# Semaphore waits between the indirect transfers of a mixture-of-experts layer on one core: the scatter waits at every second transfer, the closing gather at every tile

## The chip, the cores and the metric

The kernel runs on one core of one Trainium2 chip. The metric is the device time of one execution in microseconds (us). The engines are TensorE (PE, with its weight loads shown apart as PEld), VectorE (DVE), ScalarE (ACT), GpSimd (POOL) and SyncE (SP), which here only starts transfers.

## What is computed

One transformer layer over 2048 tokens of width 512: sparse and windowed attention, a layer norm, then a mixture of experts with a shared part, and a second layer norm. The change lies in the mixture of experts. Its reference, cut to what matters:

```python
scores = sigmoid(xf @ gate_w.T) + expert_bias          # 16 experts, 4 groups, best 2 groups kept
_, idx = top_k(masked, 4)                               # four experts per token
w = take_along_axis(original_scores, idx); w = w / sum(w)
h = silu(einsum('td,edh->teh', xf, w1)) * einsum('td,edh->teh', xf, w3)
y = einsum('teh,ehd,te->td', h, w2, cw)                 # routed experts
z = silu(xf @ sw1) * (xf @ sw3) @ sw2                   # shared experts
x = layernorm(x + y + z)
```

The kernel doesn't compute every expert for every token: it sorts the tokens by expert, computes only the picked ones and gathers the results back.

## The kernel before

The activations stand in SBUF as `acc`, 16 token tiles (NT) of 128 tokens by 512 numbers. The feed-forward part has three blocks, with a barrier of all engines after each.

**The shared experts and the routing (block that ends at line 1029).** Two shared experts of three row blocks each make six steps q per chunk c of 512 tokens (four tiles); chunks 0 to 2 are done here, numbered m = 6c + q. For each step TensorE computes two products of 12 matmuls (`up`), ScalarE a silu (line 1183), VectorE (for chunk 0 GpSimd) the product of both (`hidden`, line 1020), ScalarE and VectorE its split into a high and a low part (lines 1196 and 1026), and TensorE the third product of 12 matmuls (`down`) one step later. TensorE may not start the second half of `up` of step m before `hidden` of step m - 1 is done. Meanwhile VectorE works out the routing, and ends with `slots` (line 1352): for each token the four rows of a DRAM buffer `xs` to which it goes. Then GpSimd scatters: for each tile n and pick k, one indirect transfer (line 1229) writes the 128 rows of `acc[:, n, :]` to `xs`, 64 transfers of 256 KB. They count on one semaphore per chunk, `s_scat[0]` to `s_scat[3]`, 16 each. These wait for it:

- VectorE, before it may change `acc` of a chunk that is being sent: for chunk 0 in steps q = 2 to 5 of chunk 1 (line 1370), behind `hidden` of that step and ahead of the next one, and for chunks 1 and 2 at the end of the chunk (line 1375);
- SP, for all four, before it loads the first sorted tile (line 1049);
- GpSimd itself, for all four, before the barrier.

**The routed experts (block that ends at line 1447).** Loops over tiles of sorted tokens, expert by expert; results go to the DRAM buffer `ys`.

**The close (`combine`, block that ends at line 1651).** GpSimd gathers the four result rows of each token, four indirect transfers of 256 KB per tile (line 1716), into one of NG = 6 buffers `got`; they count on the buffer's semaphore `s_got`. VectorE adds them to `acc`, weighted (line 1762), and takes mean and variance (lines 1767 to 1771). GpSimd then raises the variance to the power -1/2 (`power`, line 1722), VectorE makes the bias of the norm from it (`less_mean`, line 1736), ScalarE applies both (line 1696) and SP stores the tile. In the same block TensorE, ScalarE and VectorE compute the shared experts of the last chunk, six steps (`late_block`) beside tiles 1 to 6, whose results VectorE adds at tiles 12 to 15 (line 1756). GpSimd's order sets the pace, since `power` stands behind gathers that run six tiles ahead, and VectorE takes tile n + 2 only after `power(n)`:

```python
for n in range(NT):
    gather(n)
    if n >= NG:
        power(n - NG)
for n in range(NT - NG, NT):
    power(n)
```

Of the kernel before, what the change touches and what calls it, by code (L numbers as in the profile page):

```python
# [31 lines left out]
TPC = CH // P  # L32
# [11 lines left out]
PICK = 4  # L44
# [892 lines left out]
def front(nc, t, bank, acc, ident, xs, zeroed, slots, pick_w, tile_expert, first_tile, neghalf, x, x_in,  # L937
# [7 lines left out]
    with st:  # L945
# [33 lines left out]
        s_scat = [sem(f"scatter_done{c}", st) for c in range(NCH)]  # L979
# [12 lines left out]
        def piece(i):  # L992

            return (i // QUARTERS + 1) % RING, quarter(i % QUARTERS)
# [16 lines left out]
        def hidden(eng, m):  # L1011
            rows = rows_of(m)
            eng.wait_ge(s_silu, m + 1)
            wait_hlo(eng, m - 1)
            if m < POOL_BLOCKS:
                eng.wait_ge(s_u3c, m + 1)
                eng.tensor_tensor(hid[0:rows, :], gate[0:rows, :], up3[0:rows, :], ALU.mult).then_inc(s_hid_pool, 1)
            else:
                eng.wait_ge(s_u3, m + 1)
                eng.tensor_tensor(hid[0:rows, :], gate[0:rows, :], b_u3[0:rows, :], ALU.mult).then_inc(s_hid_dve, 1)  # L1020

        def hidden_low(eng, m):
            rows = rows_of(m)
            wait_hid(eng, m)
            eng.wait_ge(s_hhi, m + 1)
            eng.tensor_tensor(hlo[0:rows, m % 2, :], hid[0:rows, :], hhi[0:rows, m % 2, :].bitcast(F32),
                              ALU.subtract).then_inc(s_hlo_pool if m < POOL_BLOCKS else s_hlo_dve, 1)

        with nc.Block() as block:
            @block.sync  # L1030
            def _(sp):
                def load_piece(i):
                    if i >= QUARTERS:
                        sp.wait_ge(s_wlo, i - QUARTERS + 1)
                    e = (E, E + 1, 0, 1)[i // QUARTERS]
                    q = i % QUARTERS
                    sp.dma_start(staged[:, quarter(q)], t["wexp"][e, :, quarter(q)]).then_inc(s_piece[q], 16)

                sp.dma_start(gateT[:, :, :], t["gateT"].rearrange("(k p) e -> p k e", p=P)).then_inc(g_in, 16)
                for i in range(QUARTERS):  # L1040
                    load_piece(i)
                sp.dma_start(ebias[:, :], t["ebias"].broadcast_to([P, E])).then_inc(g_in, 16)
                sp.dma_start(tri, t["tri"]).then_inc(g_in, 16)
                sp.dma_start(ramp[:, :], t["ramp"].broadcast_to([P, MAXT])).then_inc(g_in, 16)
                for i in range(QUARTERS, PIECES + QUARTERS):
                    load_piece(i)
                for c in range(NCH):
                    sp.wait_ge(s_scat[c], 16 * TPC * PICK)
                sp.dma_start(x[:, :], xs[P:2 * P, :]).then_inc(x_in, 16)
# [158 lines left out]
            @block.gpsimd  # L1208
            def _(pool):
                def piece_low(i):  # L1210
                    s, cols = piece(i)
                    pool.wait_ge(s_whi, i + 1)
                    pool.tensor_tensor(wlo[:, s, cols], staged[:, cols], whi[:, s, cols].bitcast(F32),
                                       ALU.subtract).then_inc(s_wlo, 1)

                pool.memset(neghalf[:, :], -0.5)
                for i in range(2 * QUARTERS):
                    piece_low(i)
                for m in range(POOL_BLOCKS):
                    hidden(pool, m)  # L1220
                    hidden_low(pool, m)
                    if m < QUARTERS:
                        piece_low(2 * QUARTERS + m)
                pool.wait_ge(s_slots, 1)
                for z in zeroed:
                    pool.wait_ge(*z)
                for n in range(NT):
                    for k in range(PICK):
                        pool.indirect_dma_start(xs[:, :], bass.IndirectOffsetOnAxis(ap=slots[:, n, k:k + 1], axis=0),
                                                acc[:, n, :], None, bounds_check=MAXT * P - 1,  # L1230
                                                oob_is_err=False).then_inc(s_scat[n // TPC], 16)
                for c in range(NCH):
                    pool.wait_ge(s_scat[c], 16 * TPC * PICK)

# [387 lines left out]
def combine(nc, t, bank, acc, ident, ys, slots, pick_w, mv, rstd, neghalf, stats, whi, wlo, staged, sb, sem):  # L1622
# [3 lines left out]
    with st:  # L1626
        NG = 6
# [11 lines left out]
        s_got = [sem(f"got{i}", st) for i in range(NG)]  # L1639
# [11 lines left out]
        with nc.Block() as block:  # L1651
            @block.tensor
            def _(pe):
                for k in range(KC):
                    wait_for(pe, s_xlo, k - 1)
                    for i in range(TPC):
                        mm = pe.transpose(bank[k % 2][:, i * P:(i + 1) * P], acc[:, LATE + i, k * P:(k + 1) * P],
                                          ident[:, :])
                    mm.then_inc(s_xt, 1)
                pe.wait_ge(s_xlo, KC)  # L1660
                for q in range(NB):
                    s, b = divmod(q, HB)
                    rows = hb_rows(b)
                    wait_for(pe, s_hid, q - 1)
                    for w in range(2):
                        for k in range(KC):
                            at = w13_cols(w, k)[0] + b * P
                            mm = three_products(pe, bank[2 + 2 * w + q % 2][0:rows, :],
                                                (whi[:, slot(s), at:at + rows], wlo[:, slot(s), at:at + rows]),
                                                (xhi[:, k, :], xlo[:, k, :]), k == 0, k == KC - 1)  # L1670
                    mm.then_inc(s_up, 1)
                pe.wait_ge(s_hlo, NB)
                for i in range(TPC):
                    cols = slice(i * P, (i + 1) * P)
                    for q in range(NB):
                        s, b = divmod(q, HB)
                        rows = hb_rows(b)
                        lo_, hi_ = w2_cols(b)
                        mm = three_products(pe, b_y[i][:, :], (hhi[0:rows, q, cols], hlo[0:rows, q, cols]),
                                            (whi[0:rows, slot(s), lo_:hi_], wlo[0:rows, slot(s), lo_:hi_]),  # L1680
                                            q == 0, q == NB - 1)
                    mm.then_inc(s_y, 1)
# [27 lines left out]
            @block.gpsimd  # L1710
            def _(pool):
                def gather(n):
                    if n >= NG:
                        pool.wait_ge(s_sum, PICK * (n - NG + 1))
                    for k in range(PICK):
                        pool.indirect_dma_start(got[n % NG][:, k, :], None, ys[:, :],  # L1716
                                                bass.IndirectOffsetOnAxis(ap=slots[:, n, k:k + 1], axis=0),
                                                bounds_check=MAXT * P - 1, oob_is_err=False).then_inc(s_got[n % NG], 16)

                def power(n):  # L1720
                    pool.wait_ge(s_eps, n + 1)
                    pool.tensor_tensor(rstd[:, n:n + 1], rstd[:, n:n + 1], neghalf[:, :], ALU.pow).then_inc(s_pow, 1)  # L1722
# [7 lines that stand above are left out]
# [105 lines left out]
```

## Time and profile before

| | us |
|---|---|
| median of 2 runs | 2546.36 (2545.96 to 2546.77) |
| profiled execution | 2546.89 |
| its span, first to last instruction | 2545.1 |
| scatter: first issue to end of the last | 1678.2 to 1759.9 |
| start of the routed experts | 1839.1 |
| close: first gather to end of the last | 2422.0 to 2514.2 |

The profiled execution took 0.5 us more than the median, and 1.8 us of it lie outside the span. Times in the trace count from the span's start. Busy time of an engine leaves out semaphore waits, branches and the time that a transfer takes after its issue. TensorE's matmuls are pipelined, and their ends are modelled. A bracket at the end of a row of the timeline gives the idle time of the engine before the row and what released it; "issue" and "remote" there mean that the profile shows no releaser.

### The profile page before, as it was taken

How to read it: one execution, taken by the hardware profiler on the slowest of the kernel's cores; microseconds unless marked ns; L12 is line 12 of the kernel's file. 1: busy time of each engine (PE TensorE's matmuls, PEld its weight loads, DVE VectorE, ACT ScalarE, POOL GpSimd, SP SyncE). 2: the span in 40 equal slices, each digit the busy share in tenths (PEclk: the TensorE clock that was granted, in tenths of full speed). 3: DMA queues.
4: the chain of work that ended last, by engine and by line, in shares of the span. 5: the costliest groups of instructions: out<-in, count | busy, mean ns of one | idle time of the engine just before them, and what ended most of it. 6: DMA issues, size and time to landing. Idle time of an engine off the chain costs nothing. (4 is left out here: it accounts for less than half of the span.)

```text
span 2545.1 us, 45306 instructions
## 1 busy us (share of the span) xinstructions
PE 2249.2 (88%) x13489; PEld 2022.1 (79%) x13490; DVE 1372.0 (54%) x4446; ACT 1172.1 (46%) x3726; POOL 1345.5 (53%) x1942
## 2 busy tenths in 40 slices
PE   5399999999999999999999997773999999878763
PEld 3299999899899898998999986652789998767642
DVE  4266666667666666766666682830323323343247
ACT  2166666566566665665666664310123333333211
POOL 2576666666666666666666663455011103463374
PEclk9699999999999999999999996785999999989876
DMA  3230250000000000000000002233033324554264
GB/s 117 78 150 4 79 209 18 5 20 18 5 20 20 19 4 21 18 6 19 20 18 3 1 2 74 71 124 145 30 119 109 114 78 141 173 190 139 93 180 150
DMA packets 68916, 178.29 MB, mean 70 GB/s; under 512 B 11648, under 2 KB 15296, under 8 KB 68672
## 3 DMA queue, kind: packets, MB, share of 16 engines
q1 hardware_dynamic: 36864, 85.58, 10.1%
q0 software_dynamic: 19568, 69.10, 8.3%
q10 hardware_dynamic: 12240, 20.73, 2.2%
q8 instruction: 106, 1.74, 0.3%
q14 instruction: 138, 1.13, 0.2%
HBM read 108.26 MB, written 67.13 MB: 69 GB/s over the span
## 5 line engine op out<-in xcount | busy, mean ns | idle before, releaser
L773 POOL TENSOR_TENSOR cross<-nat,rope_tables 128x128 f32<-128x128 f32 x256 | 147.9, 578 | 447.1 <-DVE nat L635 447.1
L921 PE MATMUL bank<-whi,xT_lo 128*128 128x384 f32 x1024 | 369.6, 361 | 2.5 <-ACT v L727 1.7
L922 PE MATMUL bank<-wlo,xT_hi 128*128 128x384 f32 x1024 | 347.8, 340 | 0.0
L923 PE MATMUL bank<-whi,xT_hi 128*128 128x384 f32 x1024 | 346.8, 339 | 0.0
L1473 POOL TENSOR_TENSOR ring_lo<-staged,ring_hi 128x1088 fp32r<-128x1088 f32 x48 | 121.2, 2538 | 404.9 <-ACT ring_hi L1435 401.2
L597 DVE TENSOR_TENSOR acc<-acc,bank 128x512 f32<-128x512 f32 x256 | 175.8, 687 | 227.5 <-PE bank L923 210.3
L707 ACT COPY probT<-bank 128x128 f32<-128x128 f32 (+3 forms) x256 | 109.1, 426 | 380.8 <-PE bank L549 380.8
L921 PE MATMUL bank<-ring_hi,xslo 128*128 128x352 f32 x600 | 204.1, 340 | 29.3 <-issue 27.9
L635 DVE TENSOR_TENSOR nat<-bank,bqk 128x256 f32<-128x256 f32 x256 | 108.8, 425 | 166.3 <-PE bank L923 165.1
L921 PEld LDWEIGHTS bank<-whi,xT_lo 128*128 128x128 f32 x1024 | 193.7, 189 | 3.1 <-DVE nat L635 1.9
L923 PE MATMUL bank<-ring_hi,xshi 128*128 128x352 f32 x600 | 195.7, 326 | 0.0
L922 PE MATMUL bank<-ring_lo,xshi 128*128 128x352 f32 x600 | 195.2, 325 | 0.0
L922 PEld LDWEIGHTS bank<-wlo,xT_hi 128*128 128x128 f32 x1024 | 194.2, 190 | 0.0
L923 PEld LDWEIGHTS bank<-whi,xT_hi 128*128 128x128 f32 x1024 | 193.2, 189 | 0.0
L578 PE MATMUL bank<-probT,cv 128*128 128x128 f32 x1280 | 185.0, 275 | 3.1 <-ACT probT L709 3.1
L774 POOL TENSOR_TENSOR roped<-nat,rope_tables 128x256 f32<-128x256 f32 x256 | 181.7, 710 | 0.0
L1601 DVE TENSOR_TENSOR shlo<-bank,shhi 128x256 fp32r<-128x256 f32 x76 | 32.2, 424 | 275.7 <-ACT shhi L1567 275.7
L782 POOL TENSOR_TENSOR rstd<-ssq,half 128x2 f32<-128x2 f32 x256 | 180.5, 705 | 0.0
L716 ACT ACTIVATE prob<-prob,nbias,rstd 128x256 f32<-128x256 f32 (+1 forms) x256 | 152.7, 597 | 59.3 <-DVE nbias L622 48.4
L578 PEld LDWEIGHTS bank<-probT,cv 128*128 128x128 f32 x1280 | 163.0, 192 | 3.8 <-ACT probT L709 3.8
L539 PE MATMUL bank<-ckT,qkT 128*128 128x160 f32 (+15 forms) x512 | 161.9, 398 | 0.0
L763 POOL TENSOR_TENSOR prob<-prob,share 128x256 f32<-128x256 f32 (+1 forms) x256 | 154.7, 604 | 8.8 <-issue 8.8
(295 smaller groups left out, 6356.7 us busy)
## 6 DMA issues: line engine op xcount, KB each, us to landing
staged<-in_wexp POOLq DMA_DIRECT2D x60, 544.0 KB, 5.1
slots_in<-zeros SPq DMA_DIRECT2D x41, 512.0 KB, 5.9
xslot<-slots_in SPq DMA_DIRECT2D x76, 256.0 KB
slots_out<-yslot ACTq DMA_DIRECT2D x76, 256.0 KB, 2.0
wraw<-in_wh SPq DMA_DIRECT2D x16, 768.0 KB, 4.3
staged<-in_wexp SPq DMA_DIRECT2D x20, 544.0 KB, 3.9
slots_out<-zeros SPq DMA_DIRECT2D x9, 512.0 KB, 6.0
acc<-in_x SPq DMA_DIRECT2D x4, 1024.0 KB, 13.6
```

The costliest lines, as they stand in the source:

```text
L539: pe.matmul(dst[:, 0:w], q, ckT[:, 0:w], start=True, stop=False)
L578: mm = pe.matmul(b_ctx[:, 0:P], val, pt, start=(m == 0), stop=(m == len(parts) - 1))
L597: dve.tensor_tensor(acc[:, a.tile, :], acc[:, a.tile, :], b_out[:, :], ALU.add).then_inc(s_acc, 1)
L716: act.activation(pl, pl, ACT.Exp, bias=nbias[:, a.slot, 1:2], scale=scale, accum_out=total[:, a.slot, 1:2])
L763: pool.tensor_tensor(pl, pl, share[:, a.slot, 1:2].to_broadcast(list(pl.shape)), ALU.mult)
L773: pool.tensor_tensor(cross[:, :, :], nat[:, a.two, :, 0:2 * ROT], sin, ALU.mult).then_inc(s_mult, 1)
L774: pool.tensor_tensor(roped[:, a.two, :, :], nat[:, a.two, :, 0:P], cos, ALU.mult).then_inc(s_mult, 1)
L782: pool.tensor_tensor(rstd[:, a.slot, :], ssq[:, a.slot, :], half[:, :], ALU.pow).then_inc(s_rstd, 1)
L921: pe.matmul(out, wl_, xh_, start=first, stop=False)
L922: pe.matmul(out, wh_, xl_, start=False, stop=False)
L923: return pe.matmul(out, wh_, xh_, start=False, stop=last)
L1473: pool.tensor_tensor(wlo[:, e % RING, quarter(q)], staged[stage_of(e)][:, quarter(q)], whi[:, e % RING, quarter(q)].bitcast(F32), ALU.subt ...
```

## The change

Two waits are added on GpSimd; no transfer and no computation is added, taken away or moved.

```diff
@@ -1229,6 +1229,8 @@
                         pool.indirect_dma_start(xs[:, :], bass.IndirectOffsetOnAxis(ap=slots[:, n, k:k + 1], axis=0),
                                                 acc[:, n, :], None, bounds_check=MAXT * P - 1,
                                                 oob_is_err=False).then_inc(s_scat[n // TPC], 16)
+                        if k % 2:
+                            pool.wait_ge(s_scat[n // TPC], 16 * (PICK * (n % TPC) + k + 1))
                 for c in range(NCH):
                     pool.wait_ge(s_scat[c], 16 * TPC * PICK)
 
@@ -1716,6 +1718,7 @@
                         pool.indirect_dma_start(got[n % NG][:, k, :], None, ys[:, :],
                                                 bass.IndirectOffsetOnAxis(ap=slots[:, n, k:k + 1], axis=0),
                                                 bounds_check=MAXT * P - 1, oob_is_err=False).then_inc(s_got[n % NG], 16)
+                    pool.wait_ge(s_got[n % NG], 16 * PICK * (n // NG + 1))
 
                 def power(n):
                     pool.wait_ge(s_eps, n + 1)
```

In the scatter GpSimd goes on after picks 1 and 3 of a tile only when all transfers so far of the chunk have landed: 32 waits, with at most two transfers in flight. In the close it goes on after a tile's four gathers only when they have landed: 16 waits.

## Rows read from the trace of the kernel before

**Rows 1.** The page: the span, and TensorE's busy tenths in 40 equal slices.
```profile
span 2545.1 us, 45306 instructions
...
PE   5399999999999999999999997773999999878763
```
**Rows 2.** Busy time by stage: three windows around the scatter, and the gathers.
```profile
core 0: us, PE busy (x) PEld busy (x) DVE busy (x) ACT busy (x) POOL busy (x), PEclk, DMA share, GB/s
1678.00:1700.00 22.00, 21.83 (x93) 16.43 (x91) 3.44 (x5) 2.90 (x5) 16.82 (x17) 1.00 0.50 191
1700.00:1767.00 67.00, 10.72 (x20) 5.76 (x20) 0.94 (x2) 0.60 (x1) 45.71 (x47) 0.52 0.51 192
1767.00:1839.00 72.00, 70.46 (x304) 54.88 (x304) 21.29 (x33) 12.39 (x21) 0.00 (x0) 0.97 0.00 1
2422.00:2514.00 92.00, 59.98 (x230) 45.87 (x228) 54.58 (x102) 16.77 (x25) 73.78 (x73) 0.80 0.71 203
```
**Rows 3.** Timeline: start us, us, engine, line; GpSimd's scatter and its next work.
```profile
1678.15 1.13 POOL L1229 DMA_INDIRECT slots_in<-acc,slots  x1 [10.57 <-DVE slots L1352]
1679.58 1.00 POOL L1229 DMA_INDIRECT slots_in<-acc,slots  x1 [0.30 <-issue]
...
1697.60 0.97 POOL L1229 DMA_INDIRECT slots_in<-acc,slots  x1 [0.30 <-issue]
...
1758.92 0.97 POOL L1229 DMA_INDIRECT slots_in<-acc,slots  x1 [0.30 <-issue]
1839.07 0.10 POOL L1467 MEMSET spare<- 128x2 f32 x1 [79.18 <-POOLq L1029]
```
**Rows 4.** Timeline of the other engines beside the scatter: VectorE, TensorE, SP.
```profile
1677.01 0.20 DVE L1352 CAST slots<-slot 128x64 uint32<-128x64 f32 x1
...
1700.35 0.69 DVE L1370 TENSOR_TENSOR acc<-acc,shared 128x512 f32<-128x512 f32 x1 [6.46 <-DMA slots_in<-acc,slots]
1766.75 0.69 DVE L1020 TENSOR_TENSOR raw<-raw,bank 128x512 f32<-128x512 f32 x1 [65.71 <-remote]
...
1786.97 2.47 DVE L1375 TENSOR_TENSOR acc<-acc,bank 128x512 f32<-128x512 f32 x4
1793.46 0.69 DVE L1020 TENSOR_TENSOR raw<-raw,bank 128x512 f32<-128x512 f32 x1 [4.02 <-PE bank L923]
...
1698.24 0.40 PE L923 MATMUL bank<-xhi,ring_hi 128*128 128x512 f32 x1
...
1767.49 0.79 PE L921 MATMUL bank<-xhi,ring_lo 128*128 128x512 f32 x1 [20.57 <-DVE raw L1020]
...
1761.72 0.33 SPq L1049 DMA_DIRECT2D xslot<-slots_in  x1
```
**Rows 5.** Timeline: GpSimd's end of the routed experts, TensorE's start of the close.
```profile
2413.43 2.47 POOL L1492 TENSOR_TENSOR ring_lo<-staged,ring_hi 128x1088 fp32r<-128x1088 f32 x1
...
2421.18 1.94 PE L1657 MATMUL bank<-ident,acc 128*128 128x128 f32 x8 [16.64 <-PEq L1447]
```
**Rows 6.** Timeline of the close: GpSimd, then VectorE.
```profile
2421.97 1.09 POOL L1716 DMA_INDIRECT ring_hi<-slots_out,slots  x1 [6.06 <-issue]
...
2426.01 1.01 POOL L1716 DMA_INDIRECT ring_hi<-slots_out,slots  x1 [0.30 <-issue]
...
2459.67 0.59 POOL L1722 TENSOR_TENSOR rstd<-rstd,neghalf 128x1 f32<-128x1 f32 x1
...
2431.14 3.11 DVE L1762 SCALAR_TENSOR_TENSOR acc<-ring_hi,pick_w,acc 128x512 f32<-128x512 f32 x4 [4.15 <-issue]
...
2460.30 0.16 DVE L1736 SCALAR_TENSOR_TENSOR mv<-mv,rstd 128x1 f32<-128x1 f32 x1 [18.91 <-issue]
```
**Rows 7.** The chain that ended last, in order of time: around the last gather.
```profile
2513.18 1.00 POOL ring_lo L1716
2514.20 0.59 POOL rstd L1722
```
**Rows 8.** DMA traffic from 2514.2 to 2519.0 us, in 40 slices of 0.12 us.
```profile
GB/s 478 376 307 307 171 137 68 171 171 273 68 341 273 205 239 137 171 0 0 0 119 324 427 375 410 358 171 0 0 0 0 0 0 0 0 0 0 0 0 0
```

## The prediction

> **What bounds the kernel now.** I read the page's slices first: TensorE is at 9 tenths nearly everywhere, with a weak place in slices 25 to 28 (63.6 us each, 1527 to 1781 us) and another in the last six [rows 1]. The scatter lies in slices 27 and 28, the close in the last two. Then the busy times by stage [rows 2]. From 1678 to 1700 us TensorE is full beside the scatter. From 1700 to 1767 it has 20 matmuls in 67 us, and VectorE and ScalarE do three operations together. From 1767 to 1839 it is full again, with 304 matmuls in 72 us and no traffic. So in the middle window something holds everybody, and the timeline shows that it ends soon after the scatter. GpSimd issues its 64 transfers every 1.28 us, 0.97 us each and a gap of 0.30, until 1758.92 + 0.97 = 1759.89 [rows 3]. VectorE's `hidden` of step m = 9 starts only at 1766.75 after an idle time of 65.71 us, marked "remote": no releaser is shown [rows 4]. Its input, the last product of that step's `up` on TensorE, stands in the timeline at 1698.24 [rows 4]. I don't know the mechanism. What the rows show is that TensorE's results became visible very late while transfers into DRAM were issued back to back, and that all is normal 7 us after the last of them.
>
> The routed experts start at 1839.1, when TensorE and VectorE are done; GpSimd by then has waited 79.18 us for the barrier [rows 3]. So before, the scatter's end itself is not the bound of this block: the held TensorE is. After it comes the routed stage, which is full of TensorE's work and moves as a whole with its start.
>
> In the close GpSimd is the bound. It is busy 73.78 of 92 us, the rest being the gaps of 0.3 us [rows 2], and the first `power` comes at 2459.67, behind 28 gathers; VectorE waits 18.91 us for it and goes on at 2460.30 [rows 6]. The chain of waits runs along GpSimd's gathers to 2514.20, then `power(9)`, then VectorE's last tiles [rows 7]. From the end of the last gather (2513.18 + 1.00 = 2514.18) to the span's end are 30.9 us that no wait on GpSimd changes.
>
> **First edit: a drain after every second scatter.** From the end of an issue to the moment at which another engine sees the landing:
>
> - the 16th transfer ends at 1697.60 + 0.97 = 1698.57, VectorE, which waits for the first chunk, starts at 1700.35 [rows 3, 4]: 1.78 us;
> - the 64th ends at 1759.89, SP issues its load at 1761.72: 1.83 us, of which I count 1.77 as the wait.
>
> After a wait GpSimd doesn't start a transfer at once: from the end of `slots` (1677.01 + 0.20 = 1677.21) to the first scatter (1678.15) are 0.94 us [rows 3, 4], against the gap of 0.30 back to back, since the issues' preparation otherwise runs ahead. In the close the barrier gives 0.79 us for the same thing (TensorE's start at 2421.18, GpSimd's at 2421.97) [rows 5, 6]. I take 0.94. One pair then costs 1.43 (start to start, rows 1678.15 and 1679.58) + 1.00 + 1.77 + 0.94 = 5.14 us instead of 2.56. The last wait ends at 1678.15 + 31 x 5.14 + 4.20 = 1841.7 instead of 1761.7.
>
> Behind this wait on GpSimd stands only the barrier. Before a barrier GpSimd needs time after its last work: it ends at 2413.43 + 2.47 = 2415.90 and the others start at 2421.18 [rows 5], 5.3 us. So the routed experts can't start before 1847.0, against 1839.1: **+7.9 us**.
>
> Do the engines get there sooner? The chunk semaphores come later: chunk 0 at 1678.15 + 7 x 5.14 + 4.20 = 1718.3 (now 1700.35), chunk 1 at 1759.5, chunk 2 at 1800.6. VectorE stands at chunk 0's wait ahead of `hidden` of m = 9, so TensorE stops at the second half of m = 10's `up` until about 1719.7, the point at which it now resumes at 1767.49 [rows 4]. From there the rest of the block took 71.6 us; chunk 1's wait adds about 16 (VectorE would be at line 1375 at 1739, is held to 1759.5, 2.5 us of adding follow, and its cover until the next `hidden` is 4 us: 1786.97 + 2.47 to 1793.46 [rows 4]). That gives 1807, some 35 us ahead of the scatter's end. If the holding back of TensorE goes with the pause between pairs, the block is bound by GpSimd; a part of it, up to those 35 us, could stay without moving the barrier. The stall of 67 us thus goes, and what is late next is the scatter itself. Since TensorE then idles before the barrier it starts the routed stage at half clock: after 1767.49 the granted clock is at its lower level for seven matmuls or so (0.43 against 0.23 us apart), I add **+1.4 us**.
>
> Bounds: with a restart of 0.30 instead of 0.94 a pair takes 4.50, the last wait ends at 1821.9, and the stage's start is at 1827.2, so -11.9. With a landing 0.3 us later a pair takes 5.44, and the start is at 1856, so +17.
>
> **Second edit: a drain after each tile's four gathers.** Everything here is on the chain. Four issues take 2421.97 to 2426.01 + 1.01 = 2427.02, 5.05 us [rows 6]. The landing: VectorE took tile 0 at 2431.14, 4.1 us after the fourth issue's end, with five more transfers behind it [rows 6]; the last gather, with nothing behind it, ended at 2514.18, and its data stop in slice 17 of the DMA view, at 2516.2, 2.1 us later [rows 8], to which comes what semaphore and wait take, 0.4 (in the scatter of the same size 1.77 is all of it). So 2.5 to 4.1; drained transfers are like the last, and the stores that run beside them add a little: I take 2.8. The restart is 0.9 again; where `power` stands between two tiles, its 0.6 us hides behind the restart. A tile then takes 5.05 + 2.8 + 0.9 = 8.75 us, and the gathers 15 x 8.75 + 7.85 = 139.1 instead of 92.2: **+46.9 us**. VectorE's 4 to 6 us per tile and the late step of TensorE fit in 8.75, so they stay hidden, and the last 30.9 us stay. Bounds: 2.5 and 0.3 give 7.85 per tile and +33; 4.1 and 0.9 give 10.05 and +68.
>
> A rule speaks against this order of prices. The Trainium skill ("DMA: Bandwidth & Descriptors", section on the anatomy of one DMA on the SWDGE path) says that most of a transfer's fixed 2 us is the receipt of the last write, and that this is dearest where the target is HBM. By it the scatter, which writes HBM, should land later after its issue than the gather, which writes SBUF. The rows say 1.77 us for the scatter and 2.5 or more for the gather. With the gather at the scatter's 1.77 the close would grow by 15 x 7.72 + 6.82 - 92.2 = 30.4 us instead of 46.9; I go by the rows.
>
> **Sum.** 2546.9 (profiled) + 7.9 + 1.4 + 46.9 = 2603.1; against the median, which lies 0.5 lower, 2602.6. I say 2603, 2.2% slower. A measurement of this kernel tells about 2% from no change, 51 us, so this is close to the line.
>
> **Rivals.**
>
> *Waits without restart (not slower).* If GpSimd has the next transfer prepared while it waits, the 46 restarts that follow a drain cost nothing. Pairs take 4.20, the scatter ends at 1812.6 and the stage starts at 1817.9: -21.2. The gathers take 16 x 7.55 = 120.8 with the short landing: +28.6. With the clock's 1.4 the sum is +8.8, 2556. For it: back-to-back issues do run ahead. Against it: both first issues after a wait took 0.8 to 0.94. Each 0.1 us of restart is 31 + 15 times 0.1, 4.6 us; below 0.83 us, all else as above, the sum falls under 2%.
>
> *TensorE stays held.* If any traffic of the scatter holds TensorE's results back, not its unbroken stream, it resumes only after 1841.7 + 5, and its 71.6 us follow: the stage starts near 1918, +79, with the close 2674. For it: the stall lasted as long as the scatter. Against it: from 1678 to 1700 the same traffic (191 GB/s) left TensorE full, and drained pairs leave the DMA idle for most of the time. It decides once more than half of the 67 us of stall remain.
>
> *Slow gathers.* Landings as of tile 0, 4.1 us: close +68, 2624. Against it: the last one took 2.5.
>
> **How the numbers follow.** Forecast and its surroundings 0.66, no or small restart 0.2, TensorE held 0.07, slow gathers 0.07. Eight in ten lie between 2575 (restart half as long, gathers landing in 2.5) and 2625 (slow gathers, or some stall left). Slower by over 2%: 0.52 of the forecast's 0.66 and both slow rivals, 0.66. Within 2%: 0.14 + 0.18, 0.32. Faster: 0.02, since even the free waits give +9.
>
> **What the next profile would show.** Right: pairs of scatters 5.1 us apart, no "remote" wait longer than the chunk waits, TensorE idle before a barrier at 1847, tiles of gathers 8.7 us apart, the close's end 31 us after the last issue. Wrong: a restart near 0.3, a first stage after 1860, or gathers that land under 2.2 or over 3.5 us after their last issue.

## The result, and the profile after

| | before | changed |
|---|---|---|
| median of 2 runs, us | 2546.36 | 2595.26 (2594.14 to 2596.39) |
| profiled execution, us | 2546.89 | 2596.39 |
| its span, us | 2545.1 | 2594.5 |
| start of the routed experts | 1839.1 | 1839.0 |
| close: first gather to end of the last | 2422.0 to 2514.2 | 2420.6 to 2560.3 |

The ratio is 1.019, 95% interval [1.015, 1.024]: 1.9% slower, 49 us. The median of 2595.3 lies 8 us under the forecast of 2603. In this kernel's lines everything behind the scatter stands 2 higher (1354 for 1352, 1372 for 1370, 1377 for 1375, 1469 for 1467), and everything behind the gathers 3 higher.

The page, against [rows 1]: the weak place of TensorE is now flatter and as long (slices of 64.9 us here), and its end is weaker: the last three slices stand at 4, 4 and 2 tenths instead of 7, 6 and 3.

```profile
span 2594.5 us, 45317 instructions
...
PE   5399999999999999999999979876699998898442
```

Busy time by stage, the same three windows as in [rows 2], then the gathers:

```profile
1678.00:1700.00 22.00, 22.00 (x97) 17.13 (x96) 3.39 (x5) 3.03 (x5) 9.44 (x10) 1.00 0.30 114
1700.00:1767.00 67.00, 43.87 (x178) 33.88 (x177) 14.20 (x22) 7.48 (x14) 26.24 (x27) 0.82 0.27 104
1767.00:1839.00 72.00, 33.22 (x143) 25.62 (x142) 7.98 (x12) 4.71 (x8) 26.30 (x28) 0.76 0.28 106
2421.00:2560.00 139.00, 62.80 (x228) 46.45 (x226) 55.38 (x102) 16.40 (x25) 72.22 (x73) 0.71 0.48 134
```

From 1700 to 1767 us TensorE does 178 matmuls where it did 20, and from 1767 to 1839 it does 143 where it did 304. The stall is gone, and its work has moved forward; but the stage still starts at 1839. The gathers' window is 47 us longer, with nearly the same busy time of GpSimd (72.2 and 73.8).

GpSimd's timeline of the scatter, against [rows 3]:

```profile
1677.53 1.13 POOL L1229 DMA_INDIRECT slots_in<-acc,slots  x1 [10.56 <-DVE slots L1354]
1678.96 1.00 POOL L1229 DMA_INDIRECT slots_in<-acc,slots  x1 [0.30 <-issue]
1682.51 0.97 POOL L1229 DMA_INDIRECT slots_in<-acc,slots  x1 [2.54 <-DMA slots_in<-acc,slots]
...
1687.29 0.97 POOL L1229 DMA_INDIRECT slots_in<-acc,slots  x1 [2.53 <-DMA slots_in<-acc,slots]
...
1829.14 0.97 POOL L1229 DMA_INDIRECT slots_in<-acc,slots  x1 [2.53 <-DMA slots_in<-acc,slots]
1830.41 0.97 POOL L1229 DMA_INDIRECT slots_in<-acc,slots  x1 [0.30 <-issue]
1838.96 0.10 POOL L1469 MEMSET spare<- 128x2 f32 x1 [7.57 <-POOLq L1029]
```

A pair takes 4.78 us (1682.51 to 1687.29). Of the idle 2.53 us, 1.77 is the landing as before, so the restart is 0.76: VectorE, which waits for the same landing of the first chunk, starts at 1715.21, and GpSimd at 1715.98. VectorE's timeline, against [rows 4], shows that nobody is held any longer; what it waits for are the chunk's semaphores and, at the end, the barrier:

```profile
1715.21 0.69 DVE L1372 TENSOR_TENSOR acc<-acc,shared 128x512 f32<-128x512 f32 x1 [23.30 <-DMA slots_in<-acc,slots]
1715.83 0.68 DVE L1020 TENSOR_TENSOR raw<-raw,bank 128x512 f32<-128x512 f32 x1
...
1753.43 2.48 DVE L1377 TENSOR_TENSOR acc<-acc,bank 128x512 f32<-128x512 f32 x4 [16.13 <-DMA slots_in<-acc,slots]
...
1798.58 2.48 DVE L1377 TENSOR_TENSOR acc<-acc,bank 128x512 f32<-128x512 f32 x4 [1.69 <-PE bank L923]
1839.10 0.35 DVE L1609 MEMSET shid<- 128x352 f32 x1 [38.04 <-PEq L1029]
```

`hidden` of step 9 starts at 1715.83 instead of 1766.75, and VectorE is done at 1798.58 + 2.48 = 1801.06, 38 us before the barrier opens. The scatter, which before ended 79 us ahead of the barrier, now sets it.

GpSimd's timeline of the close, against [rows 5 to 7], the first tile, the start of the second, and the last:

```profile
2420.61 1.09 POOL L1718 DMA_INDIRECT ring_hi<-slots_out,slots  x1 [6.06 <-issue]
...
2430.67 1.01 POOL L1718 DMA_INDIRECT ring_hi<-slots_out,slots  x1 [5.01 <-DMA ring_hi<-slots_out,slots]
...
2555.06 1.05 POOL L1718 DMA_INDIRECT ring_lo<-slots_out,slots  x1 [0.18 <-issue]
...
2559.32 1.00 POOL L1718 DMA_INDIRECT ring_lo<-slots_out,slots  x1 [0.30 <-issue]
2563.67 1.08 POOL L1725 TENSOR_TENSOR rstd<-rstd,neghalf 128x1 f32<-128x1 f32 x2 [3.35 <-DMA ring_lo<-slots_out,slots]
```

From the first gather of the first tile to that of the last are 134.45 us, 8.96 per tile. VectorE starts tile 0 at 2429.91, GpSimd tile 1 at 2430.67: the restart is 0.76 here too. Before, `power` followed the last gather within 0.02 us [rows 7]; now it waits 3.35 us for the landing.

The difference of the two profiled spans, 49.4 us, is then: start of the routed experts -0.1, routed stage -1.3 (581.65 us against 582.90), close from its first gather to the end of the span +50.8 (173.9 against 123.1).

### The profile page after: what moved, and what is told of

The parts are those of the page before. It is cut to its first block and busy times, and to the rows that moved or that the text cites. A ratio compares the mean times of both kernels' runs of the same rounds, so it can differ in the third digit from the quotient of the medians.

```text
span 2594.5 us, 45317 instructions
## 1 busy us (share of the span) xinstructions
PE 2248.8 (87%) x13489; PEld 2023.4 (78%) x13490; DVE 1374.5 (53%) x4446; ACT 1172.1 (45%) x3726; POOL 1344.5 (52%) x1942
```

## The experiments

The forecast had one thing taken on trust: that pauses would let TensorE go, though I did not know what held it. So the runs had two aims: to price the two edits apart, and to find what it is in the scatter that holds TensorE.

**The edits apart.** e1 has the first edit alone, e2 the second alone. The diffs are the two pieces of the change.

> The scatter's 32 waits alone, the close as before. My theory (the stall of TensorE goes, and the block is bound by the drained scatter, whose end falls where TensorE's used to be): routed experts start at 1839 us as in both kernels, the whole within 5 us of before, 2542 to 2550. Rival (the two edits act on each other, and the scatter's part is a loss that the profile of the changed kernel hides): 2555 or more.

> The close's 16 waits alone, the scatter as before. My theory (every landing after a tile's last gather and every restart lies on the chain, 16 times about 3.1 us): the whole loss of the changed kernel, 2594 to 2600, close of 174 us from the first gather to the end, and the stall of 66 us beside the scatter still there. Rival as for the scatter's waits alone: under 2590.

Measured: e1 2548.05 against 2549.66 on the same chip, ratio 0.9994 [0.9984, 1.0004]; e2 2598.67, ratio 1.0170 [1.0121, 1.0219]. So by the medians the scatter's waits are worth -1.6 us, which the interval doesn't tell from nothing, and the gathers' +49.0, together 47.4 against 48.9 for the whole change. The +49.0 is loose: three of e2's four executions took 2597 to 2602 us and one, for a reason not known, 2577, and its ratio says +43, between 31 and 56. Its trace (of 2597 us) agrees with the median: from the first gather to the end are 170.9 us (174 expected), 47.8 more than before. The loss is the close's alone. In e2 the stall stands as before:

```profile
POOL spare L1467 <- POOLq L1029: 80.9, 1, 80.9
DVE raw L1020 <- remote: 75.4, 2, 66.3
```

(The list of waits from 1674 to 1860 us: engine and line, releaser, us in total, times, longest.) In e1 the "remote" row is gone from the same list, GpSimd's wait for the barrier is down to 7.6 us, and the waits of the drain stand in their place:

```profile
POOL slots_in L1229 <- DMA slots_in<-acc,slots: 78.9, 31, 2.8
...
PE bank L1508 <- PEq L1029: 35.3, 1, 35.3
```

That the scatter's edit comes out at nothing is thus a sum of two large amounts: what its 31 waits add to the scatter, and the stall that they remove, which TensorE can use only up to the scatter's later end. A version with fewer waits should keep the one and save the other.

**Fewer waits.** e6 waits after every 12th transfer, as below. e3 waits after every 8th (with `if n % 2 and k == PICK - 1`) and e5 after every 16th (with `if n % TPC == TPC - 1 and k == PICK - 1`).

```diff
+                        if n % 3 == 2 and k == PICK - 1:
+                            pool.wait_ge(s_scat[n // TPC], 16 * (PICK * (n % TPC) + k + 1))
```

> One drain after every eighth scatter (8 waits instead of 32), close as before. If the stall needs a stream unbroken for longer than some 12 us, it stays away: group of 8 takes 7 x 1.28 + 0.97 + 2.53 = 12.5 us, the scatter is over at 1777, TensorE goes through chunk 1 without waiting, and the routed experts start near 1783, 56 us before the kernel before: 2490. If any traffic at this density holds TensorE and only long pauses cure it, the stall is there in part, and the time lies between 2500 and 2546.

> One drain after every sixteenth scatter (bursts of 20 us, 4 waits, the last of them the one that is there anyway). Theory (a burst holds TensorE's results only from about its twelfth us on, and the drain lets go what was held): up to 8 us of stall in each of the first two bursts, scatter over near 1769; routed experts between 1776 and 1790, 2483 to 2500. Rival (once begun, the hold outlasts the 2 us of a drain, and grows as in the kernel before): above 2515.

> One drain after every twelfth scatter (bursts of 15 us, 5 waits). Theory as for sixteen: almost nothing held, scatter over at 1773, routed experts at 1779, 8 us before the version that drains at every eighth: 2487. Rival as for sixteen: above 2505.

Measured: e3 2494.75, ratio 0.9783 [0.9766, 0.9799]; e5 2498.57, 0.9800 [0.9783, 0.9817]; e6 2486.74, 0.9758 [0.9742, 0.9775]. All three are some 2% faster than the kernel before. The lists of waits tell how much holding is left. e5 first, then e6; e3 has no such row.

```profile
ACT raw L1183 <- remote: 41.1, 5, 11.4
...
DVE raw L1020 <- remote: 25.1, 4, 10.1
```

```profile
ACT raw L1183 <- remote: 7.9, 1, 7.9
...
DVE raw L1020 <- remote: 5.8, 2, 2.9
```

With a wait after every 16th transfer no wait on the hold is longer than 11.4 us. Five of the nine, the four longest among them, end in the pause behind a stretch or within 1 us of it; the other four, of 2.3 to 7.5 us, end inside the next stretch. After every 12th little is left. The routed experts start at 1787.3 in e3 and at 1781.2 in e6, both bound by the scatter (TensorE idles 12.8 and 7.7 us before the barrier), and at 1791.0 in e5, bound by TensorE (GpSimd idles 25.9 us). Each expected time holds, e3's to within 5 us. In e5 more was held than expected (up to 11.4 us and in all four stretches, instead of up to 8 us in the first two), and the routed experts start 1 us behind the range given.

**Is it the unbroken stream, or the transfers issued ahead?** e4 takes four semaphores in turn and issues transfer j only when j - 4 has landed, as in the diff (transfer j counts on `s_scat[j % SDEEP]`, and whoever waits for a chunk waits for all four); e7 is the same with `SDEEP = 2`.

```diff
+        SDEEP = 4
+        s_scat = [sem(f"scatter_done{r}", st) for r in range(SDEEP)]
...
+                        j = PICK * n + k
+                        if j >= SDEEP:
+                            pool.wait_ge(s_scat[j % SDEEP], 16 * (j // SDEEP))
```

> No drain: four semaphores in turn, and GpSimd prepares transfer j only when transfer j - 4 has landed, so the transfers still follow each other every 1.28 us but never more than four are prepared ahead; close as before. Theory A (the unbroken stream of writes holds TensorE's results back): stall as before, routed experts at 1839, 2546. Theory B (the stall comes from transfers that GpSimd's sequencer has prepared far ahead, a dozen of them): no stall, scatter over at 1762, TensorE done at about 1776, routed experts near 1776, 63 us earlier: 2483.

> No drain, but only two transfers under way at any time: two semaphores in turn, transfer j is prepared when transfer j - 2 has landed. Transfers then follow each other evenly, every (0.97 + 1.77 + 0.76) / 2 = 1.75 us, 150 GB/s instead of 205, about the average rate of the version that drains at every eighth. If the mean rate of the writes is what holds TensorE, no stall: scatter over at 1790, routed experts at 1796, 2503. If the stream must stop altogether for a while (a drain), the stall is back, and since the stream is longer, routed experts start near 1867: 2575.

Measured: e4 2547.92, ratio 0.9998 [0.9989, 1.0008]; e7 2506.16, 0.9830 [0.9813, 0.9846]. e4's waits never bite: a transfer takes 0.97 + 1.77 = 2.74 us from its start to its landing, so at 1.28 us no more than three are under way anyway. The transfers come every 1.28 us as before, and the stall is as before. So e4 bounds what is prepared ahead, but changes nothing in what is under way. In the list of waits (line 1026 is `hidden` here, 1020 before):

```profile
DVE raw L1026 <- remote: 67.2, 1, 67.2
```

e7's waits bite at every second transfer. GpSimd's timeline there (line 1238 is 1229 before):

```profile
1702.27 0.97 POOL L1238 DMA_INDIRECT slots_in<-acc,slots  x1 [1.13 <-DMA slots_in<-acc,slots]
1703.67 0.97 POOL L1238 DMA_INDIRECT slots_in<-acc,slots  x1 [0.43 <-issue]
1705.78 0.97 POOL L1238 DMA_INDIRECT slots_in<-acc,slots  x1 [1.14 <-DMA slots_in<-acc,slots]
```

Two transfers in 3.51 us, 1.75 us each (1.83 in the mean of the whole scatter, with a few longer waits), and no "remote" row at all. So the stream need not stop for 2.5 us at a time; it suffices that it is thinner. Two readings of "thinner" were open: bytes per time (146 GB/s against 192), or transfers per time.

**Bytes or transfers.** e9 keeps the scatter of before and halves its bytes; it leaves out half of each sorted token's numbers.

```diff
-                        pool.indirect_dma_start(xs[:, :], bass.IndirectOffsetOnAxis(ap=slots[:, n, k:k + 1], axis=0),
-                                                acc[:, n, :], None, bounds_check=MAXT * P - 1,
+                        pool.indirect_dma_start(xs.rearrange("r (a d) -> (r a) d", a=2)[:, :], bass.IndirectOffsetOnAxis(ap=slots[:, n, k:k + 1], axis=0),
+                                                acc[:, n, :HID // 2], None, bounds_check=MAXT * P - 1,
```

> The scatter of before, with no wait added, but each transfer writes only the first 256 of a row's 512 numbers, into rows of half the length: 64 transfers of 128 KB, issued as before every 1.28 us, with the same number of rows each. Half of the sorted tokens' numbers are left out. Theory bytes (what holds TensorE's results back is how much is written per time, about 100 GB/s here, below the 145 to 170 at which it ran free): no remote wait over 5 us, the 67 us from 1700 to 1767 full of TensorE (about 290 matmuls), the scatter still ends at 1760, the routed experts start with TensorE's own end, 1774 to 1783, time about 2483 to 2490. Rival issue (it is the row count and GpSimd's unbroken issuing, whatever the size): the stall stays, remote wait over 40 us, stage start 1830 to 1842, time 2540 to 2548.

Measured: 2548.72 against 2547.98, ratio 1.0002 [0.9991, 1.0013]. The theory of bytes falls, which I had held until then. Busy time by stage and the list of waits in e9:

```profile
1700.00:1767.00 67.00, 15.14 (x27) 7.78 (x27) 0.31 (x1) 0.60 (x1) 44.83 (x46) 0.53 0.28 96
```

```profile
DVE raw L1020 <- remote: 80.5, 2, 67.8
```

At 96 GB/s and 0.28 of the DMA engines' time, less than the 146 GB/s at which e7 ran free, TensorE has 27 matmuls in 67 us. The transfers still come every 1.28 us with 128 rows each. That points at their pace.

**Pace, or the wait for a landing.** Every version so far that let TensorE go had waited for landings, which also bounds what is in flight. e11 and e12 wait for none. e11 has GpSimd do one small power after each transfer, e12 four after every 12th; the diff is e12's.

```diff
+        pause = sb("pause", [P, NT * PICK + 1], F32, st)
...
+                        if n % 3 == 2 and k == PICK - 1:
+                            for j in range(4):
+                                pool.tensor_tensor(pause[:, 4 * n + j + 1:4 * n + j + 2], pause[:, 0:1], neghalf[:, :], ALU.pow)
```

> The scatter of before at full size, with no wait for a landing at all: GpSimd does one power of a 128x1 column (0.57 to 0.59 us in the close) after each transfer, so that transfers are issued every 0.97 + 0.02 + 0.59 + 0.18 = 1.76 us instead of every 1.28. Theory pace (TensorE's results are held where transfers follow each other every 1.28 us, whatever their bytes, and not where they come every 1.76 us, landed or not): no remote wait over 3 us, scatter ends near 1791, the routed experts start near 1799, time about 2506 as with two in flight. Rival landing (a wait for the landing is what frees TensorE, since it bounds what is in flight): remote waits over 40 us, TensorE resumes only after 1791 + 7, stage start near 1870, time 2575 or so.

> As the version that drained after every twelfth transfer, but GpSimd does four powers (4 x 0.57 us = 2.3 us) there and waits for no landing: five pauses in the issuing, each nearly as long as a drain's 2.53 us. Theory pace: the pauses alone let TensorE catch up, remote waits under 12 us in all, stage start 1779 to 1784, time 2483 to 2492. Rival landing: remote waits over 40 us, stage start 1840 or later, time 2547 or more.

Measured: e11 2510.15, ratio 0.9854 [0.9838, 0.9871]; e12 2485.57, ratio 0.9760 [0.9744, 0.9777]. The rival (2575, 2547) falls in both. GpSimd's timeline of e11, then of e12:

```profile
1692.64 1.03 POOL L1231 DMA_INDIRECT slots_in<-acc,slots  x1 [0.18 <-issue]
1693.69 0.58 POOL L1234 TENSOR_TENSOR pause<-pause,neghalf 128x1 f32<-128x1 f32 x1
1694.46 1.03 POOL L1231 DMA_INDIRECT slots_in<-acc,slots  x1 [0.18 <-issue]
```

```profile
1691.81 0.97 POOL L1231 DMA_INDIRECT slots_in<-acc,slots  x1 [0.30 <-issue]
1692.79 2.13 POOL L1236 TENSOR_TENSOR pause<-pause,neghalf 128x1 f32<-128x1 f32 x4
1695.10 1.03 POOL L1231 DMA_INDIRECT slots_in<-acc,slots  x1 [0.18 <-issue]
```

In e11 most transfers come 1.82 us after the one before, 0.06 more than I had counted, and a few later still (1.87 in the mean); the routed experts start at 1803.8 instead of near 1799, and the time missed by 4 us. No "remote" row stands in its list of waits. In e12 one such row is left, 15.9 us on ScalarE in two waits; that is a little over the 12 us expected, and it costs nothing, since the routed experts start at 1779.8, the earliest of all versions. e12's pauses of 2.3 us are longer than a landing (1.77 us), so all transfers have landed in them, though nothing waits for it. Together:

| scatter | transfers | GB/s, 1700 to 1767 | matmuls there | longest "remote" | time, us |
|---|---|---|---|---|---|
| before | every 1.28 us | 192 | 20 | 65.7 | 2546 |
| e4, four in flight | every 1.28 us | 192 | 22 | 67.2 | 2547.9 |
| e9, half the bytes | every 1.28 us | 96 | 27 | 67.8 | 2548.7 |
| e7, two in flight | every 1.75 us, 1.83 in the mean | 146 | 248 | none | 2506.2 |
| e11, a pause after each | every 1.82 us, 1.87 in the mean | 140 | 244 | none | 2510.2 |
| e5, a wait after 16 | 16 at 1.28 us, then 2.5 idle | 189 | 232 | 11.4 | 2498.6 |
| e6, a wait after 12 | 12 at 1.28 us, then 2.5 idle | 177 | 293 | 7.9 | 2486.7 |
| e12, a pause after 12 | 12 at 1.28 us, then 2.3 of other work | 177 | 271 | 10.3 | 2485.6 |
| e3, a wait after 8 | 8 at 1.28 us, then 2.5 idle | 169 | 297 | none | 2494.8 |

(e7 and e11 have fewer matmuls than e3 because VectorE waits 15 to 16 us there for a chunk's semaphore, and TensorE 8 us for VectorE, not because of a hold. In e11 GpSimd is busy 59.5 of the 67 us and TensorE runs, so it isn't GpSimd's being busy that holds it.)

**The close.** e8 waits after each tile for the gathers of the tile before it (first diff), e10 waits for a tile's own gathers at every second tile (second diff):

```diff
+                    if n:
+                        pool.wait_ge(s_got[(n - 1) % NG], 16 * PICK * ((n - 1) // NG + 1))
```

```diff
+                    if n % 2:
+                        pool.wait_ge(s_got[n % NG], 16 * PICK * (n // NG + 1))
```

> In the close, GpSimd waits after each tile's four gathers for the landing of the tile before it, not of this one: the same number of waits, but each landing has four more issues (5.3 us) to hide behind. Scatter as before. My theory (what the close's waits cost is the exposed landing and restart, 3.1 us each, not the wait as such): no more than 3 us over before, 2546 to 2550. Rival (a wait costs by itself, as it stops the sequencer from preparing ahead): 2556 or more.

> The kernel before with the close drained after every second tile only (8 waits, eight transfers of 256 KB before each). Theory price per wait (each wait costs one landing and one restart beyond the gap of 0.3 us, 3.3 us or so, as with a wait per tile: 50.8 / 15 = 3.4): 7 of them on the chain and the last one's landing, +23 to +27, time 2571 to 2575. Rival backlog (the DMA lags behind GpSimd, more so the longer a stream is, so that a landing after eight takes 4.1 us and more as for tile 0 of the kernel before): idle times of 4.7 us and more at the waits, +34 and more, time 2581 or above.

Measured: e8 2547.37, ratio 1.0002 [0.9992, 1.0011]; e10 2569.25 against 2547.98, ratio 1.0083 [1.0066, 1.0100]. The wait as such is free in e8, where it finds its transfers landed (a single idle time of 0.30 us in the whole close). In e10, with eight waits, it costs 21 us, 2 under the 23 to 27 expected. GpSimd's list of waits in e10's close:

```profile
POOL rstd L1724 <- DMA ring_lo<-slots_out,slots: 6.5, 2, 3.5
...
POOL rstd L1724 <- DMA ring_hi<-slots_out,slots: 5.7, 2, 2.9
...
POOL ring_hi L1716 <- DMA staged<-slots_out,slots: 3.6, 1, 3.6
POOL staged L1716 <- DMA ring_lo<-slots_out,slots: 3.4, 1, 3.4
POOL ring_lo L1716 <- DMA ring_hi<-slots_out,slots: 3.1, 1, 3.1
POOL rstd L1724 <- DMA staged<-slots_out,slots: 2.9, 1, 2.9
```

These are 25.2 us for eight. A landing after eight gathers takes no longer than one after four (less 0.76 of restart in three of them, 2.9 us in the mean), so the rival of a growing backlog falls, and the price goes by the number of waits: 2.7 us each here, 3.0 in e2 (47.8 in the trace, over 16).

## Why the prediction was right, step by step

The forecast was 2603 against a measured 2595, on the predicted side and within the range, but its terms were off by more than the total shows. Against the profiled 2596.4 the sum is 6.7 us too high, in parts that are rounded: 8.0 in the scatter and 1.4 in the clock too much, with 1.3 by which the routed stage came out shorter, and 3.9 in the close too little. That the misses partly cancel is luck. The forecast also gave 0.66 to "slower by over 2%"; at 1.9%, with an interval of 1.5 to 2.4%, that stays undecided.

- **The close, +46.9 predicted, +50.8 measured.** Its mechanism was right: e2 and e8 together show that the price is the exposed landing and restart, on the path. The parts, per tile: landing 2.8 predicted, about 3.08 measured (ten waits ahead of a `power` sum to 30.9 us, six ahead of a gather to 22.9 with 0.76 of restart in each); restart 0.9 predicted, 0.76 measured; four issues 5.05 predicted, 4.95 to 5.25 measured, one of the four being 1.27 us instead of 1.01 in the last nine tiles. The sum is 8.96 against 8.75, +3.2 over 15 tiles, and the last tile took 8.61 against 7.85 (2555.06 to 2563.67). The first wait, 5.01 us, was the longest. As predicted, `power` (0.57, and a gap of 0.18) takes the place of the restart, and the end lies 30.8 us behind the last wait (30.9).
- **The scatter, +7.9 predicted, -0.1 measured.** This term was mis-sized. I took the first pair's spacing of 1.43 us for all pairs, though [rows 3] have 0.97 + 0.30 = 1.27 everywhere else, and 0.94 for the restart, the figure of the very first transfer. Measured are 1.28, 0.97, 1.77 and 0.76, 4.78 for a pair instead of 5.14. Over 31 pairs that is -11.2 us; two longer idle times (4.6 and 3.7 instead of 2.5) give 3.3 back. The first transfer is 0.6 earlier and the barrier took 5.8 us instead of 5.3 (1833.15 to 1838.96). That makes 1839.0 instead of 1847.0.
- **The stall goes.** Right, with the pairs' 104 GB/s, and e1 confirms it alone. "TensorE stays held" falls. TensorE was predicted to be done at 1807, 35 us ahead of the last landing; it is at 1801, 32 us ahead of it and 38 ahead of the barrier's opening. The chunk's semaphores let VectorE go at 1715.2 and 1753.4, predicted 1718.3 and 1759.5. "What is late next is the scatter itself" is what e3, e5, e6 and e12 confirm: there the routed experts start 48 to 59 us earlier and the time falls by 49 to 62.
- **The clock, +1.4.** TensorE does idle before the barrier and does start at the lower of its two levels, 1.2 GHz: its first matmuls of 352 columns are 0.29 us apart, and 0.16 before. Its granted clock from 1839 to 1850 is 0.71 against 0.97 before, in the busy times by stage, the changed kernel first:

```profile
1839.00:1850.00 11.00, 9.24 (x41) 8.03 (x42) 5.85 (x9) 3.99 (x6) 7.24 (x5) 0.71 0.64 234
1850.00:1860.00 10.00, 10.00 (x62) 9.37 (x61) 1.83 (x4) 2.94 (x7) 3.48 (x4) 1.00 0.87 297
```

```profile
1839.00:1850.00 11.00, 7.06 (x39) 6.07 (x40) 5.85 (x9) 3.98 (x6) 7.63 (x5) 0.97 0.66 234
1850.00:1860.00 10.00, 10.00 (x52) 9.04 (x51) 1.83 (x4) 2.65 (x6) 3.11 (x4) 0.86 0.83 294
```

  But it costs nothing. At full clock TensorE waited for the next tile's load, which the slower start now fills. TensorE's timeline has the same point at 1847.69 before and at 1847.72 after, before first:

```profile
1847.69 0.55 PE L1506 MATMUL bank<-ident,xslot 128*128 128x128 f32 x3 [2.09 <-DMA xslot<-slots_in]
```

```profile
1847.72 0.65 PE L1508 MATMUL bank<-ident,xslot 128*128 128x128 f32 x4
```

  The price was put on TensorE's work without asking what it would next wait for.
- **"Waits without restart" falls**: the restart is 0.76 us, in both edits. At that size it stands near the 0.83 at which I had put the line of 2%, and the result does lie at that line.
- **"Slow gathers" falls** as a case (4.25 us at tile 0 and 4.1 at tile 9, 2.7 to 3.4 at the others), but gathers do land later than scatters, 3.08 us in the mean against 1.77 (four at a time against two, and beside the close's other traffic). The rule of the Trainium skill ("DMA: Bandwidth & Descriptors", the section on the anatomy of one DMA on the SWDGE path), that a write's receipt is dearest where the target is HBM, would have had it the other way round; these measurements go against using it to compare a scatter with a gather.

What stays open is why TensorE is held. The runs narrow down on what it depends: by e9 it isn't the bytes, by e4 not transfers prepared more than four ahead, by e11 and e12 not that nothing waits for a landing. What is left is the unbroken stream of one transfer of 128 rows every 1.28 us over more than about a dozen. Its pace and the number under way were not tried apart: at 1.28 us up to three transfers are between start and landing, at 1.75 and 1.82 at most two, and a pause of 2.3 to 2.5 us is longer than a landing's 1.77. Whether it is the descriptors, the rows, or the completions that the transfers count up was not tried apart either, nor can the profile, which models the ends of matmuls, tell a late result from a late signal. Nor is a pace as such enough: the gathers of the kernel before, 128 rows every 1.31 us or little more, go on for 37 us before the first `power` comes between them, and the list of waits from 2420 to 2515 us has no "remote" row on any engine.

## What to carry to other kernels

A drain after each group of transfers costs one landing and one restart each time (2.5 us idle for this scatter, 2.8 to 4.1 for these gathers and 5.0 at the first) if the issuing engine is on the path; in the close the same wait placed one group later costs nothing (e8). Before judging such waits by the sum, price each by itself: here one edit gave back all that it cost and hid a version that is 2.4% faster, with a pause after every twelfth transfer. And where an engine idles for a reason that the profile can't name beside a stream of transfers, it is worth thinning out the stream by a few short pauses; here a wait for the landing wasn't needed for it.

## What the runs showed of the hardware that I had not expected

- A scatter issued from GpSimd every 1.28 us holds back what TensorE signals to VectorE and ScalarE, for as long as it goes on (65.7 us in the kernel before), while its own traffic uses as little as 0.28 of the DMA engines' time (e9). The timeline of ScalarE in the kernel before shows it step by step: `up` of step 9 goes from 1692.90 to 1698.24 on TensorE (24 matmuls, the twelfth at 1695.45), and ScalarE could start on its first half at 1733.81. TensorE's twelfth, then ScalarE's row:

```profile
1695.45 0.39 PE L923 MATMUL bank<-xhi,ring_hi 128*128 128x512 f32 x1
...
1733.81 0.60 ACT L1183 ACTIVATE raw<-bank 128x512 f32<-128x512 f32 x1 [40.71 <-remote]
```

- TensorE's own matmuls come late in it too, with nothing that they wait for in the profile. TensorE in the kernel before, from 1699 us:

```profile
1699.42 0.49 PE L921 MATMUL bank<-ring_hi,hlo 96*128 96x512 f32 x1
1701.51 0.39 PE L922 MATMUL bank<-ring_lo,hhi 96*128 96x512 f32 x1 [1.60 <-issue]
1702.22 0.51 PE L923 MATMUL bank<-ring_hi,hhi 96*128 96x512 f32 x1 [0.33 <-issue]
```

- The hold sets in some way into the stream, and pauses of 2.3 to 2.5 us keep it short: with one after 12 transfers no wait on it is longer than 7.9 us (e6) and 10.3 us (e12), after 16 none longer than 11.4 us (e5). The Trainium skill ("SBUF — State Buffer", the section on who interferes with whom) says that "PE and ACT never wait on anyone" and that DMA never contends with a compute engine. That is said of SBUF's ports, and these runs don't show that a port is what holds TensorE; but read as a promise that such traffic leaves TensorE alone, it doesn't hold here.
- Two things were steady: an indirect transfer starts 0.76 us after the landing that GpSimd waited for, wherever VectorE shows the same landing (1715.21 to 1715.98 in the scatter, 2429.91 to 2430.67 in the close), and where GpSimd was last the barrier took 5.3 to 5.8 us from its last event to the others' start (2415.90 to 2421.18 before, 1833.15 to 1838.96 after).
